# Second phase of a convolution, attention and feed-forward kernel: the residual z leaves TensorE, the add of t1 moves to GpSimd

## The reference, cut to what matters

```python
t = t + _L1_attn_ref(_ln_t(t), ...)          # this is t1
t = t + _L1_ffn_ref(_ln_t(t), ...)
# inside _L1_ffn_ref, x = z = _ln_t(t1); W1m, W2m, b1m, b2m are merged per batch
    h = jax.nn.relu(jnp.einsum('bsd,bfd->bsf', x, W1m) + b1m[:, None, :])
    out = jnp.einsum('bsf,bdf->bsd', h, W2m) + b2m[:, None, :]
    res = x + out
    mu = res.mean(axis=-1, keepdims=True)
    var = res.var(axis=-1, keepdims=True)
    return (res - mu) * jax.lax.rsqrt(var + LN_EPS) * lng + lnb
```

## Time and profile before

| | us |
|---|---|
| median of 3 runs | 749.96 (748.61 to 753.14) |
| the profiled execution | 750.53 |
| its span, first to last instruction | 748.5 |
| busy in the span: TensorE | 686.2 (92%) |
| VectorE | 655.6 (88%) |
| ScalarE | 648.2 (87%) |
| GpSimd | 502.9 (67%) |

### The profile page before, as it was taken

One profiled execution on the slowest core, in us unless ns is written; L12 is line 12 of the kernel. 1 busy time (PEld: TensorE's weight loads), 2 busy tenths in 40 slices (PEclk: granted clock), 3 DMA queues, 4 the chain that ended last, 5 costly groups with the idle time before them and its releaser, 6 DMA issues. The chain is left out here.

```text
span 748.5 us, 40511 instructions
## 1 busy us (share of the span) xinstructions
PE 686.2 (92%) x13218; PEld 531.7 (71%) x13218; DVE 655.6 (88%) x2487; ACT 648.2 (87%) x1860; POOL 502.9 (67%) x911
## 2 busy tenths in 40 slices
PE   3799899999999999999999999788999998999993
PEld 2567677777777777777777777675777787777772
DVE  5698999999999999999999999747898977998983
ACT  3698999999999999999999999546888876888883
POOL 2678989999999999999999998301333321333333
PEclk9999999999999999999999999989999999999997
DMA  4568766756666766666666656210222111222221
GB/s 140 109 116 135 150 125 140 160 129 138 154 137 135 155 134 136 151 139 142 140 145 141 140 128 123 57 36 2 72 85 82 72 57 30 86 70 84 84 84 70
DMA packets 200294, 82.58 MB, mean 110 GB/s; under 512 B 174028, under 2 KB 187503, under 8 KB 200184
## 3 DMA queue, kind: packets, MB, share of 16 engines
q1 hardware_dynamic: 200248, 81.98, 47.4%
HBM read 22.69 MB, written 17.30 MB: 53 GB/s over the span
## 5 line engine op out<-in xcount | busy, mean ns | idle before, releaser
L878 DVE SCALAR_TENSOR_TENSOR scores_lo<-p_a,scores_hi 128x512 f16<-128x512 f32 x256 | 174.5, 682 | 2.4 <-ACT scores_hi L764 2.2
L764 ACT ACTIVATE scores_hi<-p_a 128x512 f16<-128x512 f32 x256 | 162.4, 643 | 7.0 <-PE p_a L605 6.0
L1411 POOL TENSOR_TENSOR ffn_rstd_shift<-ffn_rstd_shift,consts 128x4 f32<-128x4 f32 x32 | 36.6, 1144 | 113.5 <-DVE ffn_rstd_shift L1369 113.5
L1238 ACT ACTIVATE h_f<-psb,merged_b_of_batch 128x512 f32<-128x512 f32 x128 | 87.3, 712 | 11.7 <-PE psb L1174 10.1
L1347 DVE TENSOR_TENSOR h_lo<-h_f,h_hi 128x512 f16<-128x512 f32 x128 | 95.6, 786 | 1.1 <-ACT h_hi L1249 1.1
L1193 PE MATMUL psb<-merged_W_of_batch,h_hi 128*128 128x128 f16 x512 | 94.3, 220 | 2.2 <-DVE h_lo L1347 1.6
L979 POOL CAST qk_parts<-qk_f 128x512 f16<-128x512 f32 x128 | 78.8, 616 | 24.3 <-issue 20.3
L1194 PE MATMUL psb<-merged_W_of_batch,h_hi 128*128 128x128 f16 x512 | 93.9, 219 | 0.0
L1195 PE MATMUL psb<-merged_W_of_batch,h_lo 128*128 128x128 f16 x512 | 93.8, 219 | 0.0
L622 PE MATMUL p_o<-v_parts,scores_hi 128*128 128x17 f16 x1024 | 90.2, 171 | 2.1 <-issue 0.4
L622 PEld LDWEIGHTS p_o<-v_parts,scores_hi 128*128 128x128 f16 x1024 | 81.2, 96 | 14.3 <-issue 10.8
(11 more groups left out here) (214 smaller groups left out, 2842.4 us busy)
## 6 DMA issues: line engine op xcount, KB each, us to landing
x_f<-in_x SPq DMA_DIRECT2D x32, 256.0 KB, 3.2
t_rows<-t SPq DMA_DIRECT2D x64, 128.0 KB, 2.7
t_back<-t_rows SPq DMA_DIRECT2D x32, 256.0 KB, 2.6
out<-out_tile SPq DMA_DIRECT2D x32, 256.0 KB, 2.0
tv_share<-in_L_ffn_tv_W SPq DMA_DIRECT2D x32, 128.0 KB, 2.2
qkT_parts<-qk_parts SPq DMA_TRANSPOSE x128, 3.1
zT_hi_lo<-z_parts SPq DMA_TRANSPOSE x64, 2.4
merged_W<-in_L_ffn_W SPq DMA_DIRECT2D x2, 256.0 KB, 4.5
```

The costliest lines, as they stand in the source:

```text
L764: nc.scalar.activation(ah[:, t % 2, cols], p_a[:, cols], ACT.Relu).then_inc(ahi_ready[eo], 1)
L878: nc.vector.scalar_tensor_tensor(al[:, t % 2, cols], p_a[:, cols], 0.0, ah[:, t % 2, cols], ALU.max, ALU.subtract).then_inc(alo_ready[eo], 1)
L1238: nc.scalar.activation(hf_[:, c, :], ps[:, c, :], ACT.Relu, bias=b1s[:, h // 2, c:c + 1], scale=1.0 / WS).then_inc(h_ready[c], 1)
```

## The change

z is no longer added by TensorE. VectorE adds t1 times the kept deviation to the PSUM result (residual) and writes rn in SBUF; stats and normalise read rn there, normalise in place. The final add of t1 goes from VectorE to GpSimd, behind gain. rn and t1b get four buffers instead of two, the skews of the late stages grow by one, all four order lists change. In the first phase the deviation goes to a tile r2 with one column for each of the 128 tiles, times 32 (WS), and the scales of z's readers follow. The scaled identity is gone.

```diff
-FFN_TENSOR_ORDER = [("up_0", 0), ("up_3", 0), ("up_1", 0), ("down_0", 1), ("down_1", 1), ("down_2", 1),
-                    ("down_3", 1), ("up_2", 0), ("turn", 3)]
-FFN_SCALAR_ORDER = [("hidden_3", 0), ("hidden_1", 0), ("hidden_hi_0", 0), ("hidden_0", 0), ("normalise", 2),
-                    ("hidden_2", 0), ("hidden_hi_2", 0), ("finish", 3)]
-FFN_VECTOR_ORDER = [("copy_b1", 0), ("stats", 2), ("hidden_lo_0", 1), ("hidden_lo_2", 1), ("add_up", 3),
-                    ("mean_var", 2), ("add_eps", 2), ("hidden_hi_1", 0), ("copy_w2", 0), ("shift", 2),
-                    ("hidden_hi_3", 0), ("hidden_lo_1", 0), ("hidden_lo_3", 0)]
-FFN_GPSIMD_ORDER = [("rsqrt", 2), ("gain", 2)]
+FFN_TENSOR_ORDER = [("up_0", 0), ("up_2", 0), ("up_1", 0), ("up_3", 0), ("down_0", 1), ("down_1", 1),
+                    ("down_2", 1), ("down_3", 1), ("turn", 4)]
+FFN_SCALAR_ORDER = [("hidden_0", 0), ("hidden_1", 0), ("hidden_hi_0", 0), ("hidden_2", 0), ("hidden_3", 0),
+                    ("hidden_hi_2", 0), ("normalise", 3), ("finish", 4)]
+FFN_VECTOR_ORDER = [("copy_b1", 0), ("stats", 2), ("copy_w2", 0), ("hidden_hi_1", 0), ("mean_var", 2),
+                    ("hidden_lo_0", 0), ("add_eps", 2), ("hidden_lo_1", 0), ("hidden_hi_3", 0), ("residual", 1),
+                    ("shift", 2), ("hidden_lo_2", 0), ("hidden_lo_3", 0)]
+FFN_GPSIMD_ORDER = [("rsqrt", 2), ("gain", 3), ("add_up", 3)]
...
-                                             scale=st2[:, t % 4, 8:9]).then_inc(z_ready, 1)
+                                             scale=r2[:, bass.ds(n, 1)]).then_inc(z_ready, 1)
...
-                        nc.vector.tensor_scalar(st2[:, t % 4, 9:10], st2[:, t % 4, 7:8], EPS, None, ALU.add)\
+                        nc.vector.tensor_scalar(st2[:, t % 4, 9:10], st2[:, t % 4, 7:8], EPS, 1.0 / (WS * WS), ALU.add, ALU.mult)\
...
-                        nc.vector.tensor_scalar(st2[:, t % 4, 10:11], st2[:, t % 4, 6:7], -1.0, st2[:, t % 4, 8:9],
+                        nc.vector.tensor_scalar(st2[:, t % 4, 10:11], st2[:, t % 4, 6:7], -1.0, r2[:, bass.ds(n, 1)],
...
-                        nc.gpsimd.tensor_tensor(s[:, 8:9], s[:, 9:10], mhalf, ALU.pow).then_inc(rstd2, 1)
+                        nc.gpsimd.tensor_tensor(r2[:, bass.ds(n, 1)], st2[:, t % 4, 9:10], mhalf, ALU.pow).then_inc(rstd2, 1)
...
-            t1b = sb(pb, "t1_back", [P, 2, HALF, C])
-            rn = sb(pb, "normed", [P, 2, HALF, C])
+            t1b = sb(pb, "t1_back", [P, HB, HALF, C])
+            rn = sb(pb, "normed", [P, HB, HALF, C])
...
-                for slot in range(NG * NQ, NG * NQ + HB - 1):
+                for slot in range(NG * NQ, NG * NQ + HB):
...
-                    load(0, 0)
-                    load(0, 1)
-                    with sp.Fori(1, B) as b:
-                        for hf in range(2):
-                            load(b, hf)
-                            store(b - 1, hf)
+                    for h in range(HB):
+                        load(0, h)
+                    with sp.Fori(1, B // 2) as pair:
+                        for h in range(HB):
+                            load(pair, h)
+                            store(pair - 1, h)
...
-                                at_least(pe, n_ready, q - 1)
-                            mm(o, zh[:, bass.ds(q * HALF + j, 1), :].rearrange("p a c -> p (a c)"), ident_ws[:, :], start=True, stop=False)
-                            mm(o, zl[:, bass.ds(q * HALF + j, 1), :].rearrange("p a c -> p (a c)"), ident_ws[:, :], start=False, stop=False)
-                            mm(o, ohb[:, bb, :], b2s[:, :], start=False, stop=False)
+                                at_least(pe, res_ready, q - 1)
+                            mm(o, ohb[:, bb, :], b2s[:, :], start=True, stop=False)
...
                         act.wait_ge(fsh, q + 1)
-                        at_least(act, t_done, q - 1)
                         for j in range(HALF):
-                            last = nc.scalar.activation(rn[:, hf, j, :], ps[:, 4 + hf, j * P:(j + 1) * P], ACT.Identity,
+                            last = nc.scalar.activation(rn[:, h, j, :], rn[:, h, j, :], ACT.Identity,
...
+                    def residual(g, pair, h):
+                        q, hf = HB * pair + h, h % 2
+                        dve.wait_ge(f2_done, q + 1)
+                        dve.wait_ge(t1_loaded[h], 16 * (pair + 1))
+                        at_least(dve, t_done, q - HB + 1)
+                        for j in range(HALF):
+                            last = nc.vector.scalar_tensor_tensor(
+                                rn[:, h, j, :], t1b[:, h, j, :], r2[:, bass.ds(HALF * q + j, 1)],
+                                ps[:, 4 + hf, j * P:(j + 1) * P], ALU.mult, ALU.add)
+                        last.then_inc(res_ready, 1)
+
                     def stats(g, pair, h):
                         q, hf = HB * pair + h, h % 2
-                        dve.wait_ge(f2_done, q + 1)
+                        dve.wait_ge(res_ready, q + 1)
                         for j in range(HALF):
-                            last = nc.vector.bn_stats(rs[:, hf, j, :], ps[:, 4 + hf, j * P:(j + 1) * P])
+                            last = nc.vector.bn_stats(rs[:, hf, j, :], rn[:, h, j, :])
...
-                    def add_up(g, pair, h):
-                        q, hf = HB * pair + h, h % 2
-                        dve.wait_ge(gain_ready, q + 1)
-                        dve.wait_ge(t1_loaded[hf], 16 * (2 * pair + h // 2 + 1))
-                        nc.vector.tensor_tensor(rn[:, hf, :, :], rn[:, hf, :, :], t1b[:, hf, :, :], ALU.add)\
-                            .then_inc(v_ready, 1)
...
+                    def add_up(g, pair, h):
+                        q = HB * pair + h
+                        pool.wait_ge(gain_ready, q + 1)
+                        nc.gpsimd.tensor_tensor(rn[:, h, :, :], rn[:, h, :, :], t1b[:, h, :, :], ALU.add)\
+                            .then_inc(v_ready, 1)
...
-                    run(pool, FFN_GPSIMD_ORDER, {"rsqrt": rsqrt, "gain": gain})
+                    run(pool, FFN_GPSIMD_ORDER, {"rsqrt": rsqrt, "gain": gain, "add_up": add_up})
```

More of the change, by code:

```diff
@@ L129, in build @@
         identh = sb(top, "ident_f16", [P, P], F16)
-        ident_ws = sb(top, "ident_f16_scaled", [P, P], F16)
+        r2 = sb(top, "rstd_of_tiles", [P, NT])
         maskb = sb(top, "mask_bf16", [P, P], BF16)
@@ L787, in gate_relu @@
                         act.wait_ge(gt_done, n + 1)
-                        nc.scalar.activation(gjunk[:, :], p_m2[:, P:2 * P], ACT.Relu, bias=gf1b[:, 0:1], scale=1.0 / WS,
+                        nc.scalar.activation(gjunk[:, :], p_m2[:, P:2 * P], ACT.Relu, bias=gf1b[:, 0:1],
+                                             scale=1.0 / (WS * WS),
                                              accum_out=ghs[:, bass.ds(n, 1)]).then_inc(gate_ready, 1)
@@ L1019, in build @@
         with ExitStack() as pb:
+            HB = 4
             g9 = sb(pb, "gate_and_one", [E + 1, B])
@@ L1047, in build @@
             b2_cleared = sem("b2_rows_cleared")
-            t1_loaded = [sem(f"t1_loaded_{i}") for i in range(2)]
+            t1_loaded = [sem(f"t1_loaded_{i}") for i in range(HB)]
             out_stored = [sem(f"out_stored_{i}") for i in range(2)]
@@ L1096, in _, with load, store @@
                 def _(sp):
[L1097 to L1105, removed]
+                    def load(pair, h):
+                        q = HB * pair + h
+                        if not isinstance(pair, int):
+                            sp.wait_ge(v_ready, q - HB + 1)
+                        sp.dma_start(t1b[:, h, :, :].rearrange("p a c -> p (a c)"), d["t1"][bass.ds(q * P, P), :])\
+                            .then_inc(t1_loaded[h], 16)
+                    def store(pair, h):
+                        b, hf = 2 * pair + h // 2, h % 2
+                        sp.wait_ge(ob_ready, HB * pair + h + 1)
                         sp.dma_start(d["out"][bass.ds(b * P, P), hf * 512:(hf + 1) * 512], ob[:, hf, :])\
                             .then_inc(out_stored[hf], 16)
-                    load(0, 0)
-                    load(0, 1)
-                    with sp.Fori(1, B) as b:
-                        for hf in range(2):
-                            load(b, hf)
-                            store(b - 1, hf)
-                    store(B - 1, 0)
-                    store(B - 1, 1)
+                    for h in range(HB):
[4 more added lines that the diff above has]
+                            store(pair - 1, h)
+                    for h in range(HB):
+                        store(B // 2 - 1, h)
                     sp.wait_ge(out_stored[0], 16 * (B + 1))
@@ L1204, in turn @@
                         for j in range(HALF):
-                            last = nc.tensor.transpose(ps[:, 6 + hf, j * P:(j + 1) * P], rn[:, hf, j, :], ident)
+                            last = nc.tensor.transpose(ps[:, 6 + hf, j * P:(j + 1) * P], rn[:, h, j, :], ident)
                         last.then_inc(t_done, 1)
```

(8 more changed lines are left out.)

10 lines of the change are left out of this document (4 added, 6 removed).

## The result

The changed kernel takes 775.38 us (median of four runs, 773.75 to 777.22), where the kernel before takes 750.75 beside it: 1.033 times as long, 95% interval 1.030 to 1.035, about 25 us slower. The forecast was 783 us, its own range 766 to 790.

A forecast was written before the change was run, and what follows sets the result against it. TensorE (6.57 us) and VectorE's loop through rsqrt (6.63) were taken to bound the 6.60 us slot. VectorE's 5.96 plus 1.77 standing made 7.73: 29 x 1.13 = 32.8 us on 750.5, about 783 us; own range 766 to 790.

The forecast's parts named there:

- The mechanism: Second phase: VectorE instructions with two SBUF inputs stand while GpSimd's gain or add reads SBUF, 1.77 us per slot.
- its data from ScalarE is there already: GpSimd's gain, queued behind rsqrt, was taken to start at once, keeping SBUF until E + 2.80; shift stands 0.68 us.
- the forecast's kind: Second-phase slot with gain right behind rsqrt, shift standing 0.68 and hidden_lo_3 1.09 us; 7.73 us in all.
- set off against each other to nothing: Outside the full slots: about +2 us at the end against 1.4 won in slots 0 to 2, taken to cancel.
- Two terms of that slot: VectorE's slot: 5.96 us of work without standing plus 1.77 us of standing, 7.73 us.
- E + 1.66: Forecast end of GpSimd's rsqrt, E being the epsilon add's start, after losing 0.40 us to hidden_lo_1.
- TensorE is thus full: Second phase before the change: TensorE busy 6.57 of a 6.60 us slot, 6.12 without the z matmuls.
- rival 2: Gain and add fall where VectorE reads at most one SBUF input; faster, 737 to 745 us; chance 0.17.
- The boundary between two h_lo: GpSimd's waiting add gets SBUF between hidden_lo_2 and hidden_lo_3, so hidden_lo_3 stands 1.09 us.
- rival 1: VectorE keeps SBUF through hidden_lo_2 and hidden_lo_3, holding the add out; 761 or 750 us; chance 0.19.
- Both rules that I weighed: Between back-to-back VectorE subtractions, either the waiting GpSimd operation gets SBUF, or VectorE keeps it through both.
- the 0.13 us of the prediction: An operation was taken to let go of SBUF 0.13 us before its recorded end.

The follow-up runs named there:

- the fills: Changed kernel with GpSimd's add cut to one column per tile, then two wide memsets that write SBUF without reading: 748.27 us.
- the early copy: Changed kernel with the bias copied half a batch earlier, so that ScalarE never waits for it: 784.08 us.
- z matmuls put back: Changed kernel with new order, GpSimd gates and bias copy behind the epsilon operation, plus the eight z matmuls per down projection again: 747.85 us.
- both operations narrow: Changed kernel with GpSimd's gain and add both cut to one column of each tile: 730.01 us.
- the last version: Changed kernel with early bias copy, new order, GpSimd waits before gain and add, and the bias copy moved behind the epsilon operation: 737.56 us.
- after: The profiled execution of the changed kernel itself, with nothing further altered; 775.38 us.
- order alone: Changed kernel with early bias copy and reordered engine queues (statistics, mean and epsilon as one block), no GpSimd waits: 779.44 us.
- the run with the add on VectorE: Changed kernel with the add of t1 back on VectorE, a slot after its gain: 764.11 us.

## Why the prediction came out as it did, point by point

- **The mechanism held.** h_lo and shift stand while GpSimd reads SBUF, the loss is nearly all there, and a GpSimd that is as busy without reading leaves the slot as it is. The Trainium skill's rule in "SBUF — State Buffer", section "Who interferes with whom", that a VectorE instruction with two SBUF inputs contends with a GpSimd one that reads SBUF and not with one that only writes it, agrees with these runs: 1.07 us of standing beside the add, h_lo at 676 ns beside the fills.
- **The step that failed** is the one in brackets, "its data from ScalarE is there already". In every second slot it isn't: ScalarE waits 3.3 us for the bias copy, normalise is late, and gain misses shift. Standing came to 1.37 us a slot and not 1.77, the slot to 7.26 and not 7.73; with that wait gone, every slot is of the forecast's kind and takes 7.69. So the slots cost 21.1 us and not 32.8; the total came nearer (25 for 33) by the 4.3 us of the other stretches, which the forecast had set off against each other to nothing. I had read which engine has what to do in a slot, but not whether ScalarE can start its slot, which hangs on a copy of four columns in VectorE's queue.
- **Two terms of that slot were mis-sized and cancelled.** With the early copy, standing is 4 x (0.941 - 0.684) + (1.142 - 0.16) = 2.01 us, because rsqrt takes 1.67 on the mean and ends at E + 1.96, not E + 1.66. The extra 0.3 fits an rsqrt kept out through the cast behind hidden_lo_1 as well: that lets go at 696.87 + 0.41 - 0.13 = 697.15, and 1.01 more is 698.16, where rsqrt ended at 698.15 (an estimate; no run moves the cast). The forecast's agreement with this run, 7.73 and 7.69, is thus in part luck. VectorE's work without standing is 7.69 - 2.01 = 5.68, not 5.96; part of that is mean_var, which no longer follows its statistics directly: 0.29 from start to start, not 0.40. Residual itself is as forecast, 1.03 to 1.04 for four against 1.08.
- **"TensorE is thus full" was wrong.** I read busy time as need. The z matmuls put back show 6.38 us with no gap, and the sum by parts gives the same: 2.60 + 60 x 0.056 + 0.44 = 6.40. So TensorE had 0.2 us to spare in each slot before, where its records show 6.57 busy; without z it needs 5.94, not 6.12. It changed no term of the forecast, since VectorE set the slot, but it made rival 2 too dear by 0.18 a slot: 730.01 with both operations narrow lies below its 737.
- **The boundary between two h_lo** went as forecast in the first kind of slot (rival 1 otherwise), and against it in the second, where gain, asking 0.05 us before hidden_lo_2 let go, was kept out through hidden_lo_3 as well. Both rules that I weighed were seen in one trace.
- **Smaller terms.** The first phase and the setup between the phases took 1.45 us more in the profiled execution (0 taken, 4.7 the bound), no more than the spread of that stretch. The end took 2.9 more (2 taken), 1.6 of it where the clock fell, which the forecast had not in it.
- **Rival 2 is real**, but only where it is put there: gain under residual and add under the statistics is what the last version has, 737.56 us. The engines don't settle so by themselves.

## What to carry to other kernels

When an operation moves to GpSimd, its duration there is not its price: list what VectorE runs beside it, count every instruction with two SBUF inputs, but also casts and tiny copies, as standing for all of its reads, expect some copies to stand even beside a GpSimd that only writes, and place it, by waits if need be, beside work on PSUM. Treat busy time of TensorE as an upper bound of its need, and work the need out from the distances between starts where nothing waits. A wait that looks harmless can be what keeps two operations apart: before removing one, ask what will meet then.

## What the runs showed of the hardware

- Instructions with one SBUF input stand too. A cast of 128x512 from float32 to float16 took 1.48 us beside GpSimd's add (0.42 else), and a copy of 128x4 took 1.23 and 1.25 us (0.15 to 0.17 else). The statistics (0.86) and residual, whose other input is in PSUM, did not. My forecast had only counted instructions with two. The Trainium skill has it in "SBUF — State Buffer", section "Who interferes with whom": copies and casts can run in a mode that takes both ports, and then contend; the durations here agree.
- Who gets SBUF between two back-to-back VectorE instructions stays open. GpSimd's operation got it where it had started 0.41 us (add, after), 0.36 and 0.34 us (gain and add, order alone) before VectorE let go, and did not where it had started 0.05 to 0.07 us before; but in the run with the add on VectorE, gain started 0.6 us before hidden_lo_2 let go and was kept out through hidden_lo_3 (2.46 us for 1.27). rsqrt, which starts 0.39 us before hidden_lo_1 lets go in after and 0.38 in the run with the early copy, seems to have got it in the one (1.38 us) and not in the other (1.72). (Times of letting go are estimates, the recorded end less the 0.13 us of the prediction.)
- GpSimd writing only, 508 columns in 0.52 us, twice a slot, did not hold up h_lo (676 ns), but it did hold up two copies of VectorE: 128x512 float16 took 554 ns and not 281, 128x128 float16 546 and not 203.
